# Two batches of a decoder, one ahead of the other through three stages, and keys and values made earlier

## The reference

```python
# decayed attention
q = relu(x @ W_q.T + b_q); k = relu(x @ W_k.T + b_k); v = x @ W_v.T + b_v
A = sigmoid(x @ W_a.T + b_a)
log_g = cumsum(log(A + 1e-06), axis=1, reverse=True)
scores = where(tril, einsum('btd,bsd->bts', q, k * exp(log_g)), 0.0)
out = einsum('bts,bsd->btd', scores, v) / (scores.sum(-1) + EPS)
# last cross attention: 16 heads of 8, keys and values from ctx (154 rows)
Q = x @ Wq.T + bq; K = ctx @ Wk.T + bk; V = ctx @ Wv.T + bv
out = softmax(where(mask, -inf, Q @ K.T / sqrt(8))) @ V @ Wo.T + bo
# gated units: 8 experts, the top 2 of a router's logits, and a shared unit
y_e = (silu(x @ wg[e].T) * (x @ wu[e].T)) @ w_down[e].T
out = shared + sum_e comb[:, e] * y_e
```

## Time and profile before

| what | value |
|---|---|
| median of three runs | 1312.2 us |
| profiled execution's own time | 1315.47 us |
| its span in the trace | 1313.7 us |
| PE busy | 1146.4 us, 87% of the span |
| DVE busy | 778.2 us, 59% |
| ACT busy | 709.0 us, 54% |
| POOL busy | 556.7 us, 42% |

### The profile page before, as it was taken

The page is one execution under the profiler, slowest core; times in us unless marked ns, Lnnn a source line. Parts: engine busy times, 40 slices in busy tenths (PEclk is TensorE's granted clock), DMA queues, the critical chain, the costliest instruction groups (busy, mean ns, idle before and its releaser), DMA issues.

```text
span 1313.7 us, 21103 instructions
## 1 busy us (share of the span) xinstructions
PE 1146.4 (87%) x7320; PEld 756.2 (58%) x7320; DVE 778.2 (59%) x2164; ACT 709.0 (54%) x1889; POOL 556.7 (42%) x643
## 2 busy tenths in 40 slices
PE   4399998989999897999989799998759995799698
PEld 2255555665556465555656556556539993454387
DVE  7776665567666647666655666655334215676466
ACT  2187665537766645776644676754334443265333
POOL 2467643457753437775335676533221001111211
PEclk8599999999999999999999899998879998799699
DMA  4000010001011000110100010010021100000011
GB/s 141 16 10 17 18 41 9 25 1 39 17 26 41 5 21 1 47 18 17 41 25 0 1 42 19 17 25 0 11 81 33 49 17 0 1 1 1 1 45 39
DMA packets 60281, 31.58 MB, mean 24 GB/s; under 512 B 34261, under 2 KB 51474, under 8 KB 60178
## 3 DMA queue, kind: packets, MB, share of 16 engines
q1 hardware_dynamic: 60177, 30.23, 8.7%
HBM read 29.06 MB, written 1.16 MB: 23 GB/s over the span
## 4 chain that ended last, share of the span: by engine, by line
PE 75%; DVE 12%; POOL 6%; ACT 4%; issue 2%; DMA 0%; SPq 0%; POOLq 0%; DVEq 0%
PE bank L1648 13%; PE bank L1625 8%; PE bank L1602 8%; PE bank L1708 7%; PE bank L1865 4%; PE bank L1676 3%; PE bank L1796 2%; PE bank L1594 2%; PE bank L1798 2%; PE bank L1797 2%; PE bank L1659 2%; PE bank L1679 2%; PE bank L1677 2%; PE bank L1972 1%; PE bank L2091 1%
## 5 line engine op out<-in xcount | busy, mean ns | idle before, releaser
L938 DVE CUSTOM_DVE_ANT_0 bank<-bank,maskrow 128x512 f32<-128x512 f32 x256 | 172.2, 715 | 101.8 <-PE bank L1602 101.6
L1346 ACT ACTIVATE probs<-bank,tops 128x512 f32<-128x512 f32 x256 | 174.4, 686 | 94.4 <-DVE tops L938 93.9
L1358 ACT ACTIVATE KA<-bank 128x512 f32<-128x512 f32 x256 | 139.2, 600 | 26.1 <-PE bank L1625 21.5
L1602 PE MATMUL bank<-QR 64*128 64x512 f32 x768 | 127.0, 438 | 16.6 <-DVE rot L927 12.1
L1625 PEld LDWEIGHTS bank<-ident,probs 128*128 128x128 f32 x1024 | 117.0, 141 | 38.7 <-issue 26.3
L1625 PE MATMUL bank<-ident,probs 128*128 128x128 f32 x1024 | 134.2, 274 | 2.3 <-ACT Vs L1318 2.3
L1648 PE MATMUL bank<-KA,Vs 128*64 128x512 f32 x512 | 135.4, 615 | 0.0
L1342 ACT ACTIVATE probs<-bank,tops 128x154 f32<-128x154 f32 x256 | 96.7, 388 | 63.2 <-DVE tops L935 61.6
L926 DVE TENSOR_TENSOR rot<-bank,cos 128x512 f32<-128x512 f32 (+1 forms) x112 | 73.6, 657 | 61.5 <-PE bank L1679 52.2
L1602 PEld LDWEIGHTS bank<-QR 64*128 64x128 f32 x768 | 65.9, 191 | 44.3 <-issue 24.3
L670 POOL TENSOR_TENSOR rstd<-var,neghalf 128x4 f32<-128x4 f32 x24 | 24.4, 1018 | 145.0 <-DVE var L985 144.7
(11 more groups left out here) (280 smaller groups left out, 2513.9 us busy)
## 6 DMA issues: line engine op xcount, KB each, us to landing
recT<-dram_r SPq DMA_DIRECT2D x56, 128.0 KB, 3.2
W<-in_W SPq DMA_DIRECT2D x8, 256.0 KB, 3.0
Vc<-in_wup SPq DMA_DIRECT2D x8, 224.0 KB, 2.5
W<-in_sWk SPq DMA_DIRECT2D x4, 256.0 KB, 4.1
W<-in_sWq SPq DMA_DIRECT2D x4, 256.0 KB, 4.2
W<-in_sWv SPq DMA_DIRECT2D x4, 256.0 KB, 4.3
wo<-in_sWo SPq DMA_DIRECT2D x4, 256.0 KB, 2.8
ck<-in_cWk SPq DMA_DIRECT2D x4, 256.0 KB, 2.8
```

The source lines that it names most:

```text
L938: v.tensor_tensor_reduce(bank[i][:, :], bank[i][:, :], maskrow[:, u.b * S:(u.b + 1) * S], -SCALE, 3.0e38, ALU.add, ALU.min, tops[:, g % 4, ...
L1346: c.activation(to, bank[i][:, :], ACT.Exp, bias=tops[:, g % 4, e, 0:1], scale=-1.0, accum_out=sums[:, n, e, k:k + 1]).then_inc(q.probs_rea ...
L1358: c.activation(turned_self(u)[:, half, :, k * P:(k + 1) * P], bank[4 + half][:, :].rearrange("p (c t) -> p c t", t=P), ACT.Copy).then_inc( ...
L1602: ins = mm(bank[first + e][:, :], QH[rows_of(e), u.j, a, w], KH[rows_of(e), u.j, c, :], start=(n == 0), stop=(n == 2))
```

## The change

Batch one goes first and batch two follows one part behind, through the decayed attention, the first steps of the last cross attention and the entry to the gated units. On VectorE the batch-one norm of the decayed attention starts between the last expert's two adds. On each engine the steps of the two batches are interleaved in a written order. The weighing uses four banks (`NUM_BANKS`) instead of two, the scores banks 5 and 6. Keys and values of the last cross attention, with the writes of constants, are made at expert 3 (`e == 3`; GpSimd's zeroes at expert 2). ScalarE loads the sigmoid table with a one-column activation ahead of the stage, and the small number is added as the bias of Ln, not by a copy. The second batch's norm, transposes and queries of the cross attention stand inside its first steps. At the gated units' entry batch one is normed, turned and multiplied with the router ahead of batch two, and `glu_products(0)` stands ahead of `route1`.

The core of the diff:

```diff
+NUM_BANKS = (7, 3, 0, 1)
+        ones_row = KA[:, 4 * NT:4 * NT + S]
...
                 low_weights(wl[e % 2], ew1[e % 2][:, :], wh[e % 2])
+                if e == 2:
+                    g.memset(Vx[:, :, :, DK:32], 0.0).then_inc(q.xpad_zero, 1)
+                    pool.wait_ge(q.xpad_zero, 2)
+                    g.memset(Vx[:, :, :, DK:DK + 1], 1.0).then_inc(q.xpad_zero, 1)
             norm_powers()
-            g.memset(Vx[:, :, :, DK:32], 0.0).then_inc(q.xpad_zero, 1)
-            pool.wait_ge(q.xpad_zero, 2)
-            g.memset(Vx[:, :, :, DK:DK + 1], 1.0).then_inc(q.xpad_zero, 1)
             norm_powers()
             last_attention()
             g2 = slice(0, GW)
+            power()
             low_weights(wl[0][:, g2], gup[0][:, g2], wh[0][:, g2])
-            norm_powers()
+            power()
             low_inputs(INPUTS["glu"])
...
                 softmax_of(logits)
+                glu_products(1)
                 beaten_by(logits)
-                glu_products(0)
                 beaten_count()
-                glu_products(1)
                 link(share(gate1, ex))
...
+            def decay_constants():
+                v.memset(V1[:, :, D:D + 1], 1.0)
+                link(v.memset(ones_row, 1.0))
...
+            def decay_queries_keys(b):
+                w = slice(b * S, (b + 1) * S)
+                for k, to in enumerate((q1T, k1T)):
+                    dve.wait_ge(q.qkv_full, see.next(q.qkv_full))
+                    v.tensor_scalar(to[:, w], bank[k][:, :], cols[:, 3 + k:4 + k], 0.0, ALU.add, ALU.max).then_inc(q.qkv_ready, 1)
...
+            def decay_keys(b):
+
+                w = slice(b * S, (b + 1) * S)
+                dve.wait_ge(q.decay_ready, see.next(q.decay_ready))
+                dve.wait_ge(q.qkv_ready, 3 * b + 2)
+                v.tensor_tensor(k1T[:, w], k1T[:, w], EX[:, w], ALU.mult).then_inc(q.keys_ready, 1)
...
+                    src = bank[5 + i % 2]
...
+                    src = bank[NUM_BANKS[t]]
...
             def decayed():
-                link(v.memset(V1[:, :, D:D + 1], 1.0))
-                link(v.memset(ones_row, 1.0))
-                for b in range(B):
-                    w = slice(b * S, (b + 1) * S)
...
-                    link(v.tensor_scalar(k1T[:, w], bank[1][:, :], cols[:, 4:5], 0.0, ALU.add, ALU.max))
-                    dve.wait_ge(q.decay_ready, see.next(q.decay_ready))
-                    v.tensor_tensor(k1T[:, w], k1T[:, w], EX[:, w], ALU.mult).then_inc(q.qkv_ready, 1)
...
+
+                decay_queries_keys(0)
+                decay_sums(0)
+                decay_values(0)
+                decay_queries_keys(1)
+                decay_keys(0)
+                decay_values(1)
+                decay_scores(0)
+                decay_sums(1)
+                decay_out(0)
+                decay_keys(1)
+                norm_stats(0, x, False)
+                decay_scores(1)
+                norm_scale(0, x, nx, False)
+                decay_out(1)
+                norm_stats(1, x, False)
...
-                for b in range(B):
+                def queries(b, src):
                     dve.wait_ge(q.xq_full, b + 1)
-                    v.tensor_scalar(QX[:, b * S:(b + 1) * S], bank[4 + b][:, :], cols[:, 6:7], float(DK) ** -0.5, ALU.add,
+                    v.tensor_scalar(QX[:, b * S:(b + 1) * S], src[:, :], cols[:, 6:7], float(DK) ** -0.5, ALU.add,
                                     ALU.mult).then_inc(q.xq_ready, 1)
+
+                queries(0, bank[4])
                 for hs in range(2):
                     maximum(hs)
+                norm_scale(1, x, nx, False)
                 for hs in range(XSTEPS):
                     main_out(hs)
                     if hs + 2 < XSTEPS:
                         maximum(hs + 2)
+                    if hs == 1:
+                        queries(1, bank[7])
...
                 divide(3, 1, bank[5])
+                norm_scale(0, x, nx, False)
                 xresidual(1, bank[0])
...
             for e in range(E):
-                gated(q.moe_down_full, q.moe_x_ready, gate0, e)
+                for b in range(B):
+                    gated_of(b, q.moe_down_full, q.moe_x_ready, gate0, e)
+                    if e == E - 1 and b == 0:
+                        norm_stats(0, x, False)
                 if e == 0:
-            for b in range(B):
-                norm_stats(b, x, False)
-            last_keys()
-            for b in range(B):
-                norm_scale(b, x, nx, False)
+                if e == 3:
+                    last_keys()
+                    last_values()
+                    decay_constants()
+            norm_scale(0, x, nx, False)
+            norm_stats(1, x, False)
+            norm_scale(1, x, nx, False)
             decayed()
-            for b in range(B):
-                norm_stats(b, x, False)
-            last_values()
-            for b in range(B):
-                norm_scale(b, x, nx, False)
             last_attention()
             norm_stats(1, x, False)
-            for b in range(B):
-                norm_scale(b, x, nx, False)
+            norm_scale(1, x, nx, False)
+            glu_products(0)
             route1()
             for e in range(E + 1):
                 if e:
...
-            inputs()
+            c.activation(sums[:, 0, 0, 0:1], neghalf[:, 0:1], ACT.Sigmoid)
+            input_of(0, 6, 1.0)
...
-                c.activation(AG[:, w], bank[3][:, :], ACT.Sigmoid, bias=cols[:, 5:6]).then_inc(q.act_step, 1)
+                c.activation(AG[:, w], bank[3 + b][:, :], ACT.Sigmoid, bias=cols[:, 5:6]).then_inc(q.act_step, 1)
                 act.wait_ge(q.act_step, see.next(q.act_step))
-                c.activation(AG[:, w], AG[:, w], ACT.Copy, bias=1.0e-6).then_inc(q.act_step, 1)
-                act.wait_ge(q.act_step, see.next(q.act_step))
-                c.activation(LG[:, w], AG[:, w], ACT.Ln).then_inc(q.log_ready, 1)
+                c.activation(LG[:, w], AG[:, w], ACT.Ln, bias=tiny[:, :]).then_inc(q.log_ready, 1)
+                if b == 0:
+                    input_of(1, 7, 1.0)
                 act.wait_ge(q.sums_ready, see.next(q.sums_ready))
                 c.activation(EX[:, w], CS[:, w], ACT.Exp).then_inc(q.decay_ready, 1)
-            inputs()
+            input_of(0, 6, 1.0)
...
+            def last_keys():
+
+                pe.wait_ge(q.w_l1, 64)
+                free(0)
+                mm(bank[0][:, 0:B * C], w1x[:, 1, :], ctxT[:, 0:B * C], start=True, stop=True).then_inc(q.xk_full, 1)
...
                     expert_down(e, b)
                 if e == 1:
                     expert_biases()
-
-            pe.wait_ge(q.w_l1, see.next(q.w_l1, 64))
-            free(0)
-            mm(bank[0][:, 0:B * C], w1x[:, 1, :], ctxT[:, 0:B * C], start=True, stop=True).then_inc(q.xk_full, 1)
-            lend([0], q.xk_ready)
-            for b in range(B):
...
+                if e == 3:
+                    last_keys()
+                    last_values_of()
+
+            def decay_projections(b):
+
+                pe.wait_ge(q.hT_ready, see.now(q.hT_ready))
+                free(3 + b)
+                mm(bank[3 + b][:, :], w1a[:, 3, :], hT_of(b), start=True, stop=True).then_inc(q.decay_full, 1)
+                lend([3 + b], q.log_ready)
...
-                pe.wait_ge(q.qkv_ready, see.now(q.qkv_ready))
+
+            def decay_scores(b):
+
+                pe.wait_ge(q.qkv_ready, 3 * b + 3)
+                pe.wait_ge(q.keys_ready, b + 1)
...
-            inputs()
+                    lend([i], q.num_ready)
+
+            input_of(0, 6)
+            decay_projections(0)
+            input_of(1, 7)
+            decay_projections(1)
             for b in range(B):
-                hT_wait(b)
+                decay_scores(b)
+                decay_weigh(b)
+
+            def last_queries(b, i):
...
+            input_of(0, 6)
+            last_queries(0, 4)
...
                 if hs + 2 < XSTEPS:
                     last_scores(hs + 2)
+                if hs == 0:
+                    input_of(1, 7)
+                if hs == 1:
+                    last_queries(1, 7)
...
-            gather(1, 6)
+            gather(1, 1)
+            input_of(0, 6)
+            first_at = see.now(q.hT_ready)
             last_out(1, 0)
...
-            inputs()
             for e in range(E + 1):
                 n = e % 2 if e < E else 2
                 for b in range(B):
+                    if e == 0:
+                        if b == 1:
+                            input_of(1, 7)
+                        pe.wait_ge(q.hT_ready, first_at + b)
+                        router_of(wr[:, 1, :], b)
                     glu_up(e, n, b)
-                    if e == 0 and b == 0:
-                        router(wr[:, 1, :])
-                    if e == 0 and b == 1:
-                        logits_turn()
+                if e == 0:
+                    logits_turn()
                 for b in range(B):
                     glu_down(e, n, b)
```

(4 more changed lines are left out.)

155 lines of the change are left out of this document (82 added, 73 removed).

## The result

| | before | after |
|---|---|---|
| median of 4 runs each, us | 1311.9 | 1297.9 |
| its runs, us | 1312.2, 1313.6, 1310.8, 1311.6 | 1300.0, 1299.6, 1294.1, 1296.2 |
| ratio after to before | | 0.9887 [0.9867, 0.9906] |
| profiled execution: time, span, us | 1315.5, 1313.7 | 1300.0, 1298.3 |
| mean granted clock of TensorE | 0.942 | 0.947 |

The change makes the kernel 14.0 us faster; 19.4 were forecast, from 1312.2 to 1292.8 us. Inside the range of 1284 to 1302 it stands in the upper third.

What follows compares the result with a forecast made beforehand. A chain of waits, no engine full, was taken to bound the 54.55 us to the first cross maximum. Terms +2.0 - 18.4 + 2.0 - 5.0 = -19.4 took the 1312.2 us median to 1292.8, range 1284 to 1302.

Steps and rivals of the forecast that it cites:

- matmuls put in at expert 3: Last cross attention's keys and values made at expert 3: +2.0 us (2.0 to 2.2), VectorE and GpSimd parts hidden.
- last add to first maximum: Decayed attention to the cross attention's first maximum: 36.1 us instead of 54.5, so -18.4 (-21.5 to -14.5).
- first cross steps: Start of cross attention, taking over batch two's scale, transposes, copy and query: +2.0 us, between 0 and 4.0.
- units' entry: Gated units' entry: mainly VectorE's order lets the third `glu_up` begin at 1254.0, not 1258.68; -5.0 us taken.
- The 3.4 and 5.1: Decayed attention: batch one's scores 3.4 us; then batch two's sums, four divisions and scaled keys 5.1 us.
- the forecast's own sum: Decayed attention's parts to the first maximum: 4.1 + 11.1 + 3.4 + 5.1 + 4.6 + 7.8 = 36.1 us.
- The forecast's own sign of being wrong: Cross attention: the forecast is wrong if TensorE's clock is 0.50 in the steps past the fourth.
- The rival at 5%: Cross attention at half clock, +15 us per 17.75 us stretch; two stretches give 1322.8 us; chance 5%.
- The full-clock rival: TensorE's clock never falls: -21.5 to the first maximum, -9.2 at the units, 1285.5 us; chance 20%.
- the bound kept without it: Decayed attention: table load counted at 1283 ns alone; a 1.4 us drain would move the lower bound to 1285.4.

Runs made afterwards that it cites:

- after again: The changed kernel run once more, unaltered, as base for the follow-up runs: 1297.8 us, ratio to before 0.9884.
- e3: Changed kernel with two extra 128x512 matmuls, results unused, behind batch one's last query, in TensorE's pause ahead of the cross steps: 1291.1 us.
- e10: Changed kernel with VectorE copying batch one's query ahead of batch two's statistics, nothing added: 1291.3 us.
- e6: Changed kernel with batch two's scaling, transposes and query back ahead of the first cross steps, as before: 1311.6 us, ratio to before 1.0009.
- e4: Changed kernel with GpSimd's low half of batch one's input ahead of batch two's power, batch two's output in another bank: 1292.6 us.
- e5: Changed kernel with cross steps and gated units' entry in the old order, keeping early keys and decayed-attention overlap: 1317.7 us, ratio to before 1.0058.
- b2: b1 plus extra matmuls, results unused, at the decayed attention's entry and ahead of the second unit's downs: 1283.8 us, ratio to before 0.9802.
- e9: Changed kernel with three extra matmuls, results unused, around the decayed attention's first transposes: 1294.4 us, ratio to before 0.9886.
- b1: Changed kernel with the two reorders of e4 and e10 together, no added work: 1289.1 us, ratio to before 0.9844.

## Why the prediction was right, and where it missed

| term | forecast | after | after again |
|---|---|---|---|
| matmuls put in at expert 3 | +2.0 | +2.1 | +2.1 |
| last add to first maximum | -18.4 | -18.4 | -17.5 |
| first cross steps | +2.0 | +3.8 | +6.6 |
| weighing to last output | in the next | +0.7 | +0.3 |
| units' entry | -5.0 | -3.1 | -5.1 |
| sum | -19.4 | -14.9 | -13.6 |

The sums leave out what lies ahead of the added matmuls. By the spans the second execution is 18.4 us shorter than before (1313.7 and 1295.3), not 13.6: its first expert starts 3.6 us sooner, and the experts without expert 3's added matmuls take 1.1 us less.

- **Experts: right.** Expert 3 takes 14.70 us between its adds and the others after it 12.62; nothing after it lengthens.
- **Decayed attention: right.** First projection +4.05 (forecast 4.1), first scores 11.8 later (11.1), to the first division 4.4 (3.4), to batch two's scores 3.9 (5.1), to its first division 4.4 (4.6), to the maximum 7.5 (7.8). The 3.4 and 5.1 are off by the same step: batch two's sums, 1.2 us, were reckoned behind batch one's first division and run ahead of it; together they are 8.3 for 8.5. As reckoned, the clock stood at half in the first projections and was full later. The milestones on the timeline, from the first division on:

```profile
1107.03 0.13 DVE L1178 TENSOR_SCALAR QA<-bank 128x1 f32<-128x1 f32 x1
...
1110.90 1.74 PE L2008 MATMUL bank<-QA 128*128 128x512 f32 x4 [3.09 <-issue]
...
1115.27 0.15 DVE L1178 TENSOR_SCALAR QA<-bank 128x1 f32<-128x1 f32 x1
...
1122.80 0.86 DVE L1224 TENSOR_REDUCE AT<-bank 128x2 f32<-128x308 f32 x2 [2.28 <-PE bank L2056]
```

- **First cross steps: the step that failed.** They were priced as work that fits beside other work, 0 to 4.0, at the full clock of the earlier trace rows. The work costs 1.4 (e3, e10). What was left out is that TensorE now enters the steps from a pause. Before, both batches' transposes and queries stood between the last pause and the steps; its timeline:

```profile
1133.28 2.14 PE L1556 MATMUL bank<-ident,nx 128*128 128x128 f32 x8 [4.08 <-DVE nx L862]
1135.22 3.42 PE L1953 MATMUL bank<-hT,ck 128*128 128x512 f32 x4
1138.48 0.43 PE L1967 MATMUL bank<-AT,identb 128*128 128x308 bf16 x2
```

  They ran at half clock (2.14 us for eight transposes, 0.60 for four at the full one), and the steps behind them at the full one. In e6 only batch two's half stands there, behind 3.74 us, and the clock did not rise. After the change nothing does: batch one's query comes ahead of the pause. This could be had from the forecast's own sum, where batch two's statistics and the query's copy are counted on VectorE (7.8 us) without asking what TensorE does meanwhile. 2.3 to 5.2 us of lower clock come on top. The forecast's own sign of being wrong, half clock past the fourth step, did not come in the first profile (L2056 takes 0.79 in the fourth step) and just came in the second (1.21 in the fifth).
- **Units' entry: right in kind, 0 to 1.9 us short.** That batch one's unit waits behind the second root on GpSimd was seen; it was not seen that this wait was the one to remove (e4). In the first profile the second unit's downs and tails at half clock, 2.04 for 1.13 and 1.78 for 1.16, take 1.5 us of what is missing.
- **The rival at 5%.** That TensorE enters at 1.2 GHz and "its small matmuls do not bring the clock back" was meant for the changed kernel. There the clock fell, but it was back by the fifth step. It is what e5 and e6 do: 29.75 us for 17.75, 12.0 more where the rival had 15. Against it stood that before, the steps came at full clock after a half-clock start; that start was both batches' transposes and queries, of which the change leaves none there. The changed kernel escapes since batch two's transposes and query stand among its steps, which the forecast had booked as a cost of 2.0.
- **The full-clock rival** was not met by any execution (1285.5; fastest 1294.1). b2, which holds the clock at the entry and in part elsewhere and mends GpSimd's order, comes to 1283.8.
- **On the two rules of the Trainium skill.** ScalarE's loads in the decayed attention after:

```profile
1092.94 0.69 ACT L1514 ACTIVATE QA<-bank,cols 128x512 f32<-128x512 f32 x1 [2.16 <-PE bank L1989]
1093.65 1.28 ACT L1516 ACT_TABLE_LOAD   x1
1094.94 0.72 ACT L1516 ACTIVATE QA<-QA,tiny 128x512 f32<-128x512 f32 x1
```

The sigmoid ends at 1093.63, the load begins at 1093.65 and Ln follows at 1094.94: the drain of about 1.4 us that the prediction cites from the Trainium skill does not show beside it, so the bound kept without it was the right one. The sentence of the Trainium skill ("TensorE: Matmul & The Clock Gate", "Loop structure matters more than you think") that back-to-back matmuls keep the engine at full rate is about an engine that has that rate, as in the steps of the kernel before (1.00 for 17.75 us). It cannot be turned round for one that comes in at half clock: in e6 TensorE was busy for 10.00 of 10.00 us at 0.50.

## What to carry to other kernels

Price a reorder twice: once as work beside other work, and once by what TensorE's clock is when the next long stretch begins; a pause of 1.8 to 3.7 us just ahead of it went with 2.3 to 12.0 us more behind it here. Work that has to be done anyway can be worth most where it stands ahead of a run of small matmuls or among them, and undoing each part of a change alone shows what carries it, which here was the part booked as a cost. An engine with idle time can still hold the chain by the order of its queue: GpSimd's low half, 1.3 us long, was worth 1.9 to 4.0 us in its stage by standing one place further ahead.

## What was not expected of the hardware

- TensorE can stay at 1.2 GHz while it is never idle: 29.75 us busy of 29.75 at a granted clock of 0.50 in e5 and in e6, with steps of 128x308 bf16, 32x308 f32 and 128x128 transposes. In the kernel before the same steps, entered at 2.4 GHz, keep 1.00 for 17.75 us.
- The same program's executions differ by their mean clock: eleven of the kernel before went from 1309.4 us at 0.950 to 1318.4 at 0.941, six of e9 from 1288.8 at 0.957 to 1305.9 at 0.946.
- More work can take less time: with two added matmuls (1.88 us together) in a pause, the stretch behind took 19.2 us instead of 24.4, in one profile of each. The same executions give no rule of when the clock falls: behind pauses of 1.1 us ahead of the steps it stayed up once (e10) and fell twice (b1, b2).
